# Indirect scatters and gathers in rounds of six with one semaphore, in a fused graph-attention and mixture-of-experts kernel

## The chip, the core and the metric

One core of a Trainium2 chip runs the whole kernel. Its engines are TensorE (matrix products), VectorE, ScalarE, GpSimd (called POOL in the profile) and the sync engine SP, which issues DMAs; all of them have queues of their own and meet only at semaphores. Matrices live in HBM or in the on-chip memory. The metric is the time of one execution on the device in microseconds; the kernel before took 1102.97 us as the median of three runs (1098.57 to 1109.63).

## The reference

The input `x` has 64 batches of 128 tokens with 128 features, float32. Four layers follow each other, each added to `x`:

1. graph attention with 8 heads over the 128 tokens of a batch, on a layer norm of `x`;
2. a shared feed-forward network plus a routed mixture of 8 experts with the best 2 kept per token, on a layer norm of `x`;
3. a second graph network (two attentions with a dense part between);
4. a feed-forward network applied to the tokens with the highest weight in each batch.

The change lies in layer 2:

```python
shared = gelu(x @ W1s + b1s) @ W2s + b2s
rw = softmax(x @ Wr)
topw, topi = top_k(rw, 2)
topw = topw / sum(topw)
...
h = gelu(einsum('bsd,edf->bsef', x, W1p) + b1p)
priv = einsum('bsef,efd->bsed', h, W2p) + b2p
routed = einsum('bsed,bse->bsd', priv, mask)
return shared + routed
```

## The kernel before

**Phases.** The phases run one after the other: setup, attention of layer 1 (ends near 275 us of the span), the experts of layer 2 (to near 647), the graph network of layer 3 (which first adds the experts' results to `x`), and the last feed-forward network. Each phase is a block: no engine starts the next phase before all have ended this one.

**Experts, in words.** The kernel doesn't compute all 8 experts for every token. It sorts the 16384 pairs of token and chosen expert into rows of a table in HBM, `rows_in`, so that each expert's rows stand together, cut into 71 tiles of 256 rows (`TILE`, `TILES`). Each tile belongs to one expert. Its rows are loaded, multiplied by that expert's two matrices, and stored in `rows_out`. Later each token fetches its two result rows.

**Scatter.** POOL fills `rows_in` (`rows_in` and `rows_out` are `slot_rows_in` and `slot_rows_out` in the profile). For each of the 64 batches `b` and both choices `c` one indirect DMA (line 1303) writes the 128 rows of 512 bytes of `xn[:, b]` to the places in `slots`: 128 scatters, numbered `n = 2 * b + c`. Semaphore `scattered[c]` counts those of choice `c`. Before scatter `n`, POOL waits until the scatter before it of the same choice has landed (line 1298), so at most two are under way. At every sixth (`IN_A_ROW`, line 1299) it waits for the other choice too, so that none is under way.

**Chunks.** Eight batches are a chunk, of which there are eight. Whenever a chunk's scatters are known to have landed, POOL runs a small memset (line 1302, the last at 1308) that raises `arrived`. The tiles are worked in an order that puts those first that need only early chunks; row 2 of `tile_table` says how many chunks a tile needs.

**Tile loop.** SP loads tile `t` (`sp_load`, line 1124) six tiles ahead (`AHEAD`), and for `t < 48` (`EARLY`) first waits for the chunks that the tile needs; at `t = 48` it waits for all eight (line 1123) and later no more. Between loads it stores finished tiles (line 1130); its queue is in order, so a wait holds back what is behind it. ScalarE fetches the expert's weights (322 KB, line 957), also about six tiles ahead. TensorE runs per tile: transpose the rows (line 1144) two tiles ahead, the up product (lines 1178 to 1180) one tile ahead, the down product (line 1202). VectorE splits and adds biases, ScalarE applies gelu. While POOL begins to scatter, TensorE works on the shared network (lines 1084 and 1092); the tile loop follows.

**Early gathers.** After its last scatter POOL fetches the result rows of the first 16 batches (`GATHERED_EARLY` chunks of 8) by 32 indirect DMAs (line 1321), with semaphores `early[c]` used as `scattered[c]` is. Before each of the two chunks it waits until the last tile that holds a row of it has been stored (line 1316). The other 96 gathers belong to the next phase (`pool_gather`, line 1597), have semaphores of their own, and are not touched by the change.

Of the kernel before, what the change touches and what calls it, by code (L numbers as in the profile page):

```python
# [14 lines left out]
BATCHES, TOKENS, D = 64, 128, 128  # L15
# [18 lines left out]
def wait(eng, sem, count):  # L34

    if isinstance(count, int) and count <= 0:
        return
    eng.wait_ge(sem, count)
# [887 lines left out]
TOPK = 2  # L926
# [9 lines left out]
CHUNK = 8  # L936
IN_A_ROW = 6
EARLY = 48
CHUNKS = BATCHES // CHUNK
# [5 lines left out]
def slot_rows(k, c, b):  # L945

    return k.xn[:, b, :] if c == 0 else k.xnT[:, (b + 2 * AHEAD * TILE // P) % BATCHES, :]
# [12 lines left out]
def experts_phase(nc, k, a):  # L960

    with ExitStack() as ctx:
        def sb(name, shape, dt=F32):
            return buffer(nc, ctx, name, shape, dt)
# [4 lines left out]
        def sem(name):  # L969
            return ctx.enter_context(nc.semaphore(name))  # L970
# [34 lines left out]
        pool_fence = sb("r_pool_fence", [P, CHUNKS])  # L1005
        EC = GATHERED_EARLY
# [25 lines left out]
        s = {n: sem("m_" + n) for n in (  # L1032
            "iota", "d", "slots", "keys", "marks", "table", "tot_ps", "pre_ps", "key_ps", "tab_ps", "arrived",
            "sh_ps", "sh_ok", "sy_ps", "sy_read", "fold",
            "tp_ps", "xh_ok", "xT_ok", "wh_ok", "wl_ok", "h_ps", "h_ok", "y_ps", "y_ok")}
        rows_kept = sem("m_rows_kept")
        scattered = [sem(f"m_scattered{p}") for p in range(2)]
        early = [sem(f"m_early{c}") for c in range(TOPK)]
        x_in = [sem(f"m_x_in{q}") for q in range(U)]
        out = [sem(f"m_out{q}") for q in range(U)]  # L1040
        READ_PREFIX = 16
# [202 lines left out]
        with nc.Block() as block:  # L1244
            @block.sync
            def _(sp):

                for e in range(EXPERTS):
                    def load(dst, src):
                        sp.dma_start(dst, src, allow_slow_non_contiguous=True).then_inc(k.experts_loaded, 16)  # L1250
                    load(k.b_experts[:, e, 0:FC], a["L0_ffn_b1p"][e].rearrange("(c p) -> p c", p=P))
                    load(k.b_experts[:, e, FC:FC + D], a["L0_ffn_b2p"][e].partition_broadcast(P))
                    load(k.w2_experts[:, e, :].rearrange("p (c n) -> p c n", c=FC),
                         a["L0_ffn_W2p"][e].rearrange("(c p) n -> p c n", p=P))

                sp.dma_start(k.expert_rows[:, :, 0:F], a["L0_ffn_W1p"]).then_inc(rows_kept, 16)
                sp.wait_ge(s["table"], 1)
                sp.dma_start(k.expert_rows[:, :, F:FETCHED].rearrange("e p n -> p e n"), k.b_experts[:])\
                    .then_inc(rows_kept, 16)
                sp.wait_ge(rows_kept, 32)  # L1260
                for t in range(AHEAD):
                    fetch_expert(sp, k, t, t)
                sp.wait_ge(s["sh_ps"], -(-H * U // GB) * FC)
                for t in range(U):
                    sp_load(sp, t)
                for t in range(TILES):
                    if t + U < TILES:
                        sp_load(sp, t + U)
                    sp_store(sp, t)
                for q in range(U):  # L1270
                    sp.wait_ge(out[q], 16 * len(range(q, TILES, U)))

            @block.gpsimd
            def _(pool):
                pool.iota(em8[:], [[1, EXPERTS]], base=-EXPERTS, channel_multiplier=0,
                          allow_small_or_imprecise_dtypes=True)
                pool.iota(k256[:], [[TILE, MAX_TILES_OF_ONE]], base=0, channel_multiplier=0,
                          allow_small_or_imprecise_dtypes=True)
                pool.iota(j_of[:], [[0, 1]], base=0, channel_multiplier=1, allow_small_or_imprecise_dtypes=True)
                pool.iota(j_end[:], [[0, 1]], base=TILE, channel_multiplier=TILE, allow_small_or_imprecise_dtypes=True)  # L1280
                pool.iota(j_start[:], [[0, 1]], base=0, channel_multiplier=TILE, allow_small_or_imprecise_dtypes=True)
                pool.iota(tile_far[:], [[1, TILES]], base=-int(FAR), channel_multiplier=0,
                          allow_small_or_imprecise_dtypes=True)
                pool.iota(order[:], [[1, EXPERTS]], base=0, channel_multiplier=EXPERTS,
                          allow_small_or_imprecise_dtypes=True)
                pool.iota(is_tile[:, EXPERTS, :], [[1, TILES]], base=0, channel_multiplier=0,
                          allow_small_or_imprecise_dtypes=True)
                pool.memset(payload[:, EXPERTS, 0:1], 0.0)
                pool.memset(payload[:, EXPERTS, 1:2], 1.0 / J)
                pool.memset(payload[:, EXPERTS, 2:3], 0.0)  # L1290
                pool.tensor_copy(tri_b[:], k.tri[:])
                pool.tensor_copy(ones_b[:], k.ones[:]).then_inc(s["iota"], 1)

                pool.wait_ge(k.slots_zeroed, 16 * k.zero_dmas)
                pool.wait_ge(s["slots"], 1)
                for n in range(TOPK * BATCHES):
                    b, c = n // TOPK, n % TOPK
                    wait(pool, scattered[c], 16 * b)
                    if n % IN_A_ROW == 0:
                        wait(pool, scattered[1 - c], 16 * b)  # L1300
                    if c == 0 and b % CHUNK == 1 and b > 1:
                        pool.memset(pool_fence[:, b // CHUNK - 1:b // CHUNK], 0.0).then_inc(s["arrived"], 1)
                    pool.indirect_dma_start(  # L1303
                        k.rows_in, bass.IndirectOffsetOnAxis(ap=k.slots[:, c, b:b + 1], axis=0),
                        k.xn[:, b, :], None).then_inc(scattered[c], 16)
                for c in range(TOPK):
                    pool.wait_ge(scattered[c], 16 * BATCHES)
                pool.memset(pool_fence[:, CHUNKS - 1:CHUNKS], 0.0).then_inc(s["arrived"], 1)

                pool.wait_ge(s["table"], 1)  # L1310
                for n in range(TOPK * CHUNK * EC):
                    b, c = n // TOPK, n % TOPK
                    if n % (TOPK * CHUNK) == 0:
                        at = b // CHUNK
                        stored = pool.value_load(last_at[at:at + 1, 0:1], min_val=1 + U, max_val=TILES + U)
                        pool.wait_ge(s["y_ok"], stored)
                        pool.tensor_tensor(gather_fence[:, at:at + 1], k.ones[:, 0:1], k.ones[:, 0:1], ALU.mult)
                    wait(pool, early[c], 16 * b)
                    if n % IN_A_ROW == 0:
                        wait(pool, early[1 - c], 16 * b)  # L1320
                    pool.indirect_dma_start(
                        slot_rows(k, c, b), None, k.rows_out,
                        bass.IndirectOffsetOnAxis(ap=k.slots[:, c, b:b + 1], axis=0)).then_inc(early[c], 16)
                for c in range(TOPK):
                    pool.wait_ge(early[c], 16 * CHUNK * EC)

            @block.scalar
            def _(act):
# [991 lines left out]
def build(nc, a, out):  # L2320

    with ExitStack() as whole:
        k = persistent(nc, whole)
        with ExitStack() as tokens:
            add_token_buffers(nc, tokens, k)
            with ExitStack() as buffers:
                add_attention_buffers(nc, buffers, k)
                setup_phase(nc, k, a)
                head_attention_phase(nc, k, a)
            with ExitStack() as buffers:  # L2330
                add_expert_buffers(nc, buffers, k)
                experts_phase(nc, k, a)
            combine_graph_phase(nc, k)
        last_ffn_phase(nc, k, out)
# [28 lines left out]
```

## Time and profile before

| what | value |
|---|---|
| median of three runs | 1102.97 us |
| lowest, highest run | 1098.57, 1109.63 us |
| profiled execution, whole time | 1114.18 us |
| its span, first to last instruction | 1112.5 us |
| TensorE busy in the span | 974.8 us (88%) |
| POOL busy in the span | 479.2 us (43%) |
| mean granted TensorE clock | 0.957 |

The profile is one execution of its own, and its times add up to its own total, which lies 11.2 us over the median of the three runs. Of that total, 1.7 us lie outside the span. An engine's busy time counts only instructions that work; semaphore waits show up as idle time before the next instruction. An indirect DMA appears on POOL with the time that POOL spends on issuing it, not with the time until its rows have landed; the landing shows in the wait of whoever needed it.

### The profile page before, as it was taken

How to read it: one execution, taken by the hardware profiler on the slowest of the kernel's cores; microseconds unless marked ns; L12 is line 12 of the kernel's file. 1: busy time of each engine (PE TensorE's matmuls, PEld its weight loads, DVE VectorE, ACT ScalarE, POOL GpSimd, SP SyncE). 2: the span in 40 equal slices, each digit the busy share in tenths (PEclk: the TensorE clock that was granted, in tenths of full speed). 3: DMA queues.
4: the chain of work that ended last, by engine and by line, in shares of the span. 5: the costliest groups of instructions: out<-in, count | busy, mean ns of one | idle time of the engine just before them, and what ended most of it. 6: DMA issues, size and time to landing. Idle time of an engine off the chain costs nothing. (4 is left out here: it accounts for less than half of the span.)

```text
span 1112.5 us, 25145 instructions
## 1 busy us (share of the span) xinstructions
PE 974.8 (88%) x7933; PEld 818.3 (74%) x7981; DVE 738.6 (66%) x2240; ACT 677.5 (61%) x1670; POOL 479.2 (43%) x477
## 2 busy tenths in 40 slices
PE   1699999897999999999899957998888998459998
PEld 1578888886677799999899934665556665349997
DVE  4689899885550155554455545788778896569998
ACT  4446666754433456666566625887677787367773
POOL 2556555551155654444444225666656312011111
PEclk9989999997999999999999978999999999679999
DMA  7902222112623146766576510111101000001111
GB/s 201 376 7 115 115 113 113 72 40 79 178 87 105 46 131 201 204 206 194 170 209 202 150 33 24 32 32 29 32 22 35 9 1 1 1 1 38 29 38 48
DMA packets 93001, 103.45 MB, mean 93 GB/s; under 512 B 16480, under 2 KB 69856, under 8 KB 90720
## 3 DMA queue, kind: packets, MB, share of 16 engines
q1 hardware_dynamic: 73232, 59.71, 16.5%
q10 hardware_dynamic: 11472, 25.63, 8.1%
q0 software_dynamic: 8192, 16.79, 5.0%
q8 instruction: 55, 0.90, 0.3%
q14 instruction: 50, 0.41, 0.1%
HBM read 52.54 MB, written 43.27 MB: 86 GB/s over the span
## 5 line engine op out<-in xcount | busy, mean ns | idle before, releaser
L1303 POOL DMA_INDIRECT slot_rows_in<-xn_all,slots x128 | 128.5, 1004 | 136.7 <-DMA slot_rows_in<-xn_all,slots 87.8
L1189 ACT ACTIVATE s_hT<-s_hp,expert 128x256 f32<-128x256 f32 x284 | 114.0, 474 | 72.0 <-PE s_hp L1180 51.2
L1202 PE MATMUL s_yp<-w_experts,s_hT 128*128 x1136 | 139.5, 276 | 1.7 <-issue 1.6
L1202 PEld LDWEIGHTS s_yp<-w_experts,s_hT 128*128 128x128 f32 x1136 | 133.8, 193 | 2.3 <-issue 2.3
L1210 DVE TENSOR_TENSOR xnT_all<-s_yp,expert 128x256 f32<-128x256 f32 x71 | 30.1, 423 | 117.3 <-PE s_yp L1202 87.2
L489 DVE SCALAR_TENSOR_TENSOR l_mi<-l_sbc,mT 128x512 bf16<-128x512 f32 x128 | 84.2, 668 | 5.7 <-PE l_sbc L480 5.0
L1178 PE MATMUL s_hp<-e_xh,e_wh 128*128 128x256 f32 x284 | 86.3, 304 | 0.0
L1101 ACT ACTIVATE s_hT<-s_hp,b_shared 128x512 f32<-128x512 f32 x64 | 44.0, 687 | 65.1 <-PE s_hp L1084 61.8
L1180 PE MATMUL s_hp<-e_xh,e_wl 128*128 128x256 f32 x284 | 80.7, 284 | 0.0
L1179 PE MATMUL s_hp<-e_xl,e_wh 128*128 128x256 f32 x284 | 80.6, 284 | 0.0
L1668 PE MATMUL g_hh<-w_fc,g_r1T 128*128 128x257 f32 x256 | 65.3, 402 | 14.5 <-ACT g_h L1683 9.0
L1767 POOL TENSOR_TENSOR g_u<-g_t,g_r1T 128x1024 f32<-128x1024 f32 x16 | 42.0, 2628 | 70.0 <-DVE g_t L1762 70.0
L1668 PEld LDWEIGHTS g_hh<-w_fc,g_r1T 128*128 128x128 f32 x256 | 48.1, 197 | 27.5 <-ACT g_h L1683 13.3
L1597 POOL DMA_INDIRECT xn_all<-slot_rows_out,slots x48 | 49.0, 1022 | 41.7 <-SPq L2026 23.7
L2161 POOL TENSOR_TENSOR f_wd<-f_wb,ident 128x512 f32<-128x512 f32 x16 | 21.3, 1329 | 100.4 <-ACT f_wb L2155 100.4
L1092 PEld LDWEIGHTS s_yp<-w_shared,s_hT 128*128 128x128 f32 x512 | 59.4, 192 | 6.3 <-issue 6.2
L1160 ACT CAST e_wh<-expert 128x512 fp32r<-128x512 f32 x71 | 44.0, 621 | 28.5 <-issue 28.1
L1084 PE MATMUL s_hp<-xnT_all,w_shared 128*128 128x512 f32 x128 | 59.6, 611 | 1.8 <-PEq L89 1.6
L1092 PE MATMUL s_yp<-w_shared,s_hT 128*128 128x128 f32 x512 | 60.0, 275 | 0.0
L2206 PE MATMUL f_yp<-w_last,f_hT 128*128 128x128 f32 x512 | 59.6, 275 | 0.0
L2206 PEld LDWEIGHTS f_yp<-w_last,f_hT 128*128 128x128 f32 x512 | 58.4, 192 | 0.1
L1597 POOL DMA_INDIRECT xnT_all<-slot_rows_out,slots x48 | 47.7, 994 | 18.6 <-issue 10.7
(336 smaller groups left out, 2689.4 us busy)
## 6 DMA issues: line engine op xcount, KB each, us to landing
expert<-expert_rows ACTq DMA_DIRECT2D x65, 322.0 KB
slot_rows_in<-zeros SPq DMA_DIRECT2D x9, 1024.0 KB, 12.4
xnT_all<-slot_rows_in SPq DMA_DIRECT2D x71, 128.0 KB
slot_rows_out<-xnT_all SPq DMA_DIRECT2D x71, 128.0 KB
slot_rows_out<-zeros SPq DMA_DIRECT2D x8, 1024.0 KB, 4.4
xn_all<-l_xr SPq DMA_DIRECT2D x16, 256.0 KB
xnT_all<-l_rT SPq DMA_DIRECT2D x16, 256.0 KB
out_dram<-f_ot SPq DMA_DIRECT2D x16, 256.0 KB, 2.3
```

What stands on the lines that cost most here:

```text
L489: ins = dve.scalar_tensor_tensor(mi[:, b % 2, 4 * h:4 * h + 4, :], sbc[:, h, :].rearrange("p (q i) -> p q i", q=4), 0.0, k.mT[:].unsqueeze ...
L1084: pe.matmul(hp[:, c, :], k.w1_shared[:, c * P:(c + 1) * P], k.xnT[:, bass.ds(g * GB, GB), :], start=True, stop=True).then_inc(s["sh_ps"], 1)
L1092: ins = pe.matmul(yp[p][:, b * P:(b + 1) * P], s_hT[p][:, c, b * P:(b + 1) * P], k.w2_shared[:, c, :], start=(c == 0 and b == 0), stop=(c ...
L1178: pe.matmul(out_c, wh[q % 2][:, at], xh[q % 2][:], start=True, stop=False)
L1179: pe.matmul(out_c, wh[q % 2][:, at], xl[q % 2][:], start=False, stop=False)
L1180: pe.matmul(out_c, wl[q % 2][:, at], xh[q % 2][:], start=False, stop=True).then_inc(s["h_ps"], 1)
L1189: nc.scalar.activation(hT[q % 2][:, c, :], hp[:, c, 0:TILE], ACT.Gelu, bias=wt[q][:, F + c:F + c + 1]).then_inc(s["h_ok"], 1)
L1202: ins = pe.matmul(yp[q % 2][:, h * D:(h + 1) * D], hT[q % 2][:, c, h * P:(h + 1) * P], w2, start=(c == 0 and h == 0), stop=(c == FC - 1), ...
L1303: pool.indirect_dma_start(k.rows_in, bass.IndirectOffsetOnAxis(ap=k.slots[:, c, b:b + 1], axis=0), k.xn[:, b, :], None).then_inc(scattered ...
L1597: pool.indirect_dma_start(slot_rows(k, c, b), None, k.rows_out, bass.IndirectOffsetOnAxis(ap=k.slots[:, c, b:b + 1], axis=0))\
L1668: ins = pe.matmul(hh[:, b % 2, 0:W1C], r1T[p][:, c, b * P:(b + 1) * P], k.w_fc[:, c, 0:W1C], start=(c == 0), stop=(c == H1 - 1))
L2206: ins = pe.matmul(yp[p][:, b * P:(b + 1) * P], hT[p][:, c, b * P:(b + 1) * P], k.w2_last[:, c, :], start=(c == 0 and b == 0), stop=(c == F ...
```

## The change

The two semaphores per kind become one: `scattered` for all scatters, `early` for all early gathers. The wait before each DMA for its predecessor of the same choice goes away. What is left is one wait ahead of every sixth DMA, for all that were issued before it. So up to six are under way, and then none. The memset that raises `arrived` is now run at the first of these waits at which the chunk is complete: ahead of scatters 18, 36, 48, 66, 84, 96 and 114, in place of 18, 34, 50, 66, 82, 98 and 114. The count of DMAs, their sizes, addresses and order stay the same, and so does everything outside the experts' phase.

```diff
@@ -1034,8 +1034,7 @@
             "sh_ps", "sh_ok", "sy_ps", "sy_read", "fold",
             "tp_ps", "xh_ok", "xT_ok", "wh_ok", "wl_ok", "h_ps", "h_ok", "y_ps", "y_ok")}
         rows_kept = sem("m_rows_kept")
-        scattered = [sem(f"m_scattered{p}") for p in range(2)]
-        early = [sem(f"m_early{c}") for c in range(TOPK)]
+        scattered, early = sem("m_scattered"), sem("m_early")
         x_in = [sem(f"m_x_in{q}") for q in range(U)]
         out = [sem(f"m_out{q}") for q in range(U)]
         READ_PREFIX = 16
@@ -1293,18 +1292,19 @@
 
                 pool.wait_ge(k.slots_zeroed, 16 * k.zero_dmas)
                 pool.wait_ge(s["slots"], 1)
+                arrived = 0
                 for n in range(TOPK * BATCHES):
                     b, c = n // TOPK, n % TOPK
-                    wait(pool, scattered[c], 16 * b)
                     if n % IN_A_ROW == 0:
-                        wait(pool, scattered[1 - c], 16 * b)
-                    if c == 0 and b % CHUNK == 1 and b > 1:
-                        pool.memset(pool_fence[:, b // CHUNK - 1:b // CHUNK], 0.0).then_inc(s["arrived"], 1)
+                        wait(pool, scattered, 16 * n)
+                        if n >= (arrived + 1) * TOPK * CHUNK:
+                            pool.memset(pool_fence[:, arrived:arrived + 1], 0.0).then_inc(s["arrived"], 1)
+                            arrived += 1
                     pool.indirect_dma_start(
                         k.rows_in, bass.IndirectOffsetOnAxis(ap=k.slots[:, c, b:b + 1], axis=0),
-                        k.xn[:, b, :], None).then_inc(scattered[c], 16)
-                for c in range(TOPK):
-                    pool.wait_ge(scattered[c], 16 * BATCHES)
+                        k.xn[:, b, :], None).then_inc(scattered, 16)
+                assert arrived == CHUNKS - 1
+                pool.wait_ge(scattered, 16 * TOPK * BATCHES)
                 pool.memset(pool_fence[:, CHUNKS - 1:CHUNKS], 0.0).then_inc(s["arrived"], 1)
 
                 pool.wait_ge(s["table"], 1)
@@ -1315,14 +1315,12 @@
                         stored = pool.value_load(last_at[at:at + 1, 0:1], min_val=1 + U, max_val=TILES + U)
                         pool.wait_ge(s["y_ok"], stored)
                         pool.tensor_tensor(gather_fence[:, at:at + 1], k.ones[:, 0:1], k.ones[:, 0:1], ALU.mult)
-                    wait(pool, early[c], 16 * b)
                     if n % IN_A_ROW == 0:
-                        wait(pool, early[1 - c], 16 * b)
+                        wait(pool, early, 16 * n)
                     pool.indirect_dma_start(
                         slot_rows(k, c, b), None, k.rows_out,
-                        bass.IndirectOffsetOnAxis(ap=k.slots[:, c, b:b + 1], axis=0)).then_inc(early[c], 16)
-                for c in range(TOPK):
-                    pool.wait_ge(early[c], 16 * CHUNK * EC)
+                        bass.IndirectOffsetOnAxis(ap=k.slots[:, c, b:b + 1], axis=0)).then_inc(early, 16)
+                pool.wait_ge(early, 16 * TOPK * CHUNK * EC)
 
             @block.scalar
             def _(act):
```

## Rows read from the trace of the kernel before

**Rows 1.** The page, its first line.

```profile
span 1112.5 us, 25145 instructions
```

**Rows 2.** Busy time by stretch: stretch, length, busy us per engine.

```profile
340.00:380.00 40.00, 40.00 (x224) 28.52 (x223) 4.15 (x6) 17.03 (x26) 23.09 (x25) 1.00 0.17 54
...
470.00:520.00 50.00, 49.76 (x436) 49.59 (x435) 25.77 (x58) 31.31 (x73) 22.89 (x23) 1.00 0.71 206
```

**Rows 3.** Waits of TensorE from 380 to 647: total us, times, longest.

```profile
PE s_yp L1202 <- issue: 1.6, 3, 1.1
PE r_prefix L1144 <- DVE e_xl L1153: 1.4, 2, 1.1
```

**Rows 4.** Line 1303, the scatters: durations in ns min/median/max, then idle before them.

```profile
L1303 POOL DMA_INDIRECT slot_rows_in<-xn_all,slots x128: 952/958/2168, 299.3 to 550.1; - x128
...
  DMA slot_rows_in<-xn_all,slots: 87.8, 54
```

**Rows 5.** Timeline of POOL, first round of six: start, us, what, [idle before <-releaser].

```profile
299.29 1.21 POOL L1303 DMA_INDIRECT slot_rows_in<-xn_all,slots  x1 [22.73 <-DVE slots L1436]
...
305.85 0.96 POOL L1303 DMA_INDIRECT slot_rows_in<-xn_all,slots  x1 [0.30 <-issue]
308.84 0.96 POOL L1303 DMA_INDIRECT slot_rows_in<-xn_all,slots  x1 [2.03 <-DMA slot_rows_in<-xn_all,slots]
```

**Rows 6.** Timeline of POOL, scatters beside the tile loop.

```profile
414.68 0.96 POOL L1303 DMA_INDIRECT slot_rows_in<-xn_all,slots  x1 [0.59 <-issue]
...
465.29 1.46 POOL L1303 DMA_INDIRECT slot_rows_in<-xn_all,slots  x1 [0.30 <-issue]
469.02 0.95 POOL L1303 DMA_INDIRECT slot_rows_in<-xn_all,slots  x1 [2.27 <-DMA slot_rows_in<-xn_all,slots]
...
537.74 0.95 POOL L1303 DMA_INDIRECT slot_rows_in<-xn_all,slots  x1 [2.76 <-DMA slot_rows_in<-xn_all,slots]
```

**Rows 7.** Timeline of POOL, last fence of the scatters, last early gather, next phase.

```profile
552.40 0.10 POOL L1308 MEMSET r_pool_fence<- 128x1 f32 x1 [1.38 <-DMA slot_rows_in<-xn_all,slots]
...
623.63 0.94 POOL L1321 DMA_INDIRECT xnT_all<-slot_rows_out,slots  x1 [0.30 <-issue]
648.29 0.94 POOL L1597 DMA_INDIRECT xn_all<-slot_rows_out,slots  x1 [23.71 <-SPq L2026]
```

**Rows 8.** Waits of the sync engine's own queue, whole span.

```profile
SPq L1123 <- POOL r_pool_fence L1308: 4.4, 1, 4.4
```

**Rows 9.** Timeline of the sync engine, the load of tile 48 and the next.

```profile
552.73 0.37 SPq L1124 DMA_DIRECT2D xnT_all<-slot_rows_in  x1
...
555.34 0.07 SPq L1124 DMA_DIRECT2D xnT_all<-slot_rows_in  x1
```

**Rows 10.** The page, DMA issues: count, KB each, us from issue to landing.

```profile
slot_rows_out<-zeros SPq DMA_DIRECT2D x8, 1024.0 KB, 4.4
...
out_dram<-f_ot SPq DMA_DIRECT2D x16, 256.0 KB, 2.3
```

**Rows 11.** Timeline of TensorE, the row transposes of tiles 44, 45, 46 and 48.

```profile
541.15 0.38 PE L1144 MATMUL r_prefix<-ident,xnT_all 128*128 128x128 f32 x2
...
548.48 0.41 PE L1144 MATMUL r_prefix<-ident,xnT_all 128*128 128x128 f32 x2 [1.12 <-DVE e_xl L1153]
...
553.48 0.38 PE L1144 MATMUL r_prefix<-ident,xnT_all 128*128 128x128 f32 x2
...
560.42 0.41 PE L1144 MATMUL r_prefix<-ident,xnT_all 128*128 128x128 f32 x2
```

**Rows 12.** Timeline of TensorE, the row transpose of tile 2.

```profile
395.82 0.41 PE L1144 MATMUL r_prefix<-ident,xnT_all 128*128 128x128 f32 x2 [1.07 <-issue]
```

**Rows 13.** Timeline of TensorE, the row transposes of tiles 69 and 70.

```profile
632.54 0.38 PE L1144 MATMUL r_prefix<-ident,xnT_all 128*128 128x128 f32 x2
...
635.97 0.38 PE L1144 MATMUL r_prefix<-ident,xnT_all 128*128 128x128 f32 x2
```

**Rows 14.** DMA queues from 420 to 552: packets, MB, share of 16 engines.

```profile
q0 software_dynamic: 1920, 3.94, 8.5%
```

## The prediction

> **What bounds the kernel now.** I first asked whether POOL, the only engine whose instructions change, is on the path that sets the end. The span [rows 1] is made of stages, so I read the busy times by stretch. Before the tile loop (340 to 380 us), while POOL scatters, TensorE is busy for all 40.00 us; beside the tile loop (470 to 520) for 49.76 of 50 [rows 2]. In both, POOL does about 23 us of issuing and otherwise waits. Next the waits of TensorE over the whole stretch from 380 to 647: the two groups that stand here, of three, are 1.6 and 1.4 us in all, and neither has POOL or a scatter as its releaser [rows 3]. So the experts' phase runs at TensorE's pace, one tile per 3.43 us (635.97 less 632.54 [rows 13]).
>
> Then POOL itself. Its scatters take 0.96 us each to issue and it waits 87.8 us for earlier ones to land [rows 4]. They end with the fence at 552.40. The 32 early gathers follow, the last issued at 623.63. After that POOL idles 23.71 us until the next phase starts at 648.29 [rows 7]. This gap is what the argument rests on: a POOL that finishes sooner only waits longer, since the next phase needs TensorE's last tile and the last store, not POOL.
>
> There are two places at which someone could feel the scatters: the load of tile 48, which waits for all chunks, and contention among DMAs.
>
> **What the change does to the scatters.** Unhindered issues follow each other at 0.96 + 0.30 = 1.26 us [rows 5]. In the first round no wait but the sixth's matters: from 299.29 to 308.84, 9.55 us [rows 5]. Such a round is already what the change makes of every round, so it gains nothing there. Later the two-in-flight wait costs: from 414.68 (scatter 66) to 537.74 (scatter 120) nine rounds take 123.06 us, 13.67 each [rows 6].
>
> With six in a row a round is five steps of 1.26, 6.30 us, and then the time from the sixth issue to the first of the next round. Quiet, that is 308.84 − 305.85 = 2.99 us [rows 5]; beside the tile loop 469.02 − 465.29 = 3.73 us, with two under way [rows 6]. How long it takes with six under way, no row shows. Bounds: at 2.99 a round is 9.29 us and the scatters end at 299.29 + 21.3 rounds, about 498 us; if six in flight drain no faster in total than two, nothing is gained and they end at 552. I take the loaded row, since that is the stretch where the waits are: 6.30 + 3.73 = 10.03 us. The first eleven rounds (299.29 to 414.68, 10.49 each) at 9.55 end at 404; the other 10.3 rounds at 10.03 end at **508 us**, some 44 us sooner. By the Trainium skill (DMA: Bandwidth & Descriptors, "Anatomy of one DMA — SWDGE (gpsimd) path") a DMA issued from GpSimd costs a fixed 2.0 us plus its bytes at 436 GB/s, 2.15 us for these 64 KB, counted from its issue. That would put a round at 8.45 us and the end near 480; the quiet row shows 2.99 and the loaded one 3.73, more than the page allows, and the trace decides.
>
> **The early gathers.** 32 of them are 5.3 rounds. From 552.40 to 623.63 they take 71.2 us, 2.2 each, like the loaded scatters [rows 7]. At 10 to 13.7 us per round they take 53 to 73 us and can start at 508, so POOL is done between 561 and 581 in place of 625, unless the wait for a stored tile holds them. POOL's gap before 648.29 grows from 24 to between 67 and 87 us. None of it reaches the end: **0 us**. What hides it is the rest of the tile loop; that cover would go only if POOL were later than today by 23 us.
>
> **Waits removed and added.** About 160 semaphore waits go from POOL's stream; at most part of the 0.30 us between issues, off the path: 0. The added wait stands at the head of each round. Queued behind it are the round's six issues and at times a fence. The fences of chunks 2 and 5 come two scatters later in number (at 36 and 84, 34 and 82 before), 2.5 us of issuing; two others come earlier. But scatter 36 now comes at 299.29 + 6 × 9.55 = 356.6 us, and the late rounds are 3.6 us shorter each, so no fence is later in time. On SP only one wait for a fence shows at all, the one for all chunks [rows 8], so the earlier ones have slack. SP's stores behind it are needed only six tiles later. DMAs: same number, same bytes, same order; their queues are not passed by any other.
>
> **The load of tile 48.** SP waits 4.4 us for the last fence [rows 8] and issues the load at 552.73 [rows 9]; TensorE transposes that tile at 560.42 [rows 11]. In this execution there is room, because TensorE had just lost time: from 541.15 to 553.48, two tiles take 12.33 us in place of 6.86, a stall of 5.47 us [rows 11] whose releaser isn't POOL. Without that stall tile 48 would be due at 541.15 + 4 × 3.43 = 554.87. The load's landing isn't shown. The nearest rows are 2.3 us for 256 KB and 4.4 us for 1 MB [rows 10]; so it lands at 555.0 to 557.1, that is 0.2 to 2.3 us late. In an execution without the stall the change thus saves 0.2 to 2.3 us; with it about 0 (it can't lose, as the fence comes earlier). I take 1 us, near the smaller transfer. After the change the load goes out at its own time, 552.73 − 4.4 = 548.3 or sooner.
>
> **Sum.** Profiled execution: 1114.18 − 0 (scatters) − 0 (gathers) − 0 (waits) − 0 to 1 (tile 48) = 1113 to 1114. It stands 11.2 us over the median, of which the stall may be 5.5. On the median: 1102.97 − 1 = **1102 us**.
>
> **Rivals.** *The slow scatters cause TensorE's lost time.* Between tile 2 at 395.82 [rows 12] and tile 70 at 635.97 [rows 13] lie 68 steps, 240.15 us; at 3.43 they are 233.2, so 6.9 us are lost. If all of it hangs on late rows, it goes: 1103 − 6.9 = 1096; with a lucky run more. For it: the largest loss, 5.47 us, lies in the last rounds of the scatters. Against it: no row of TensorE's waits names one, and SP's only wait for a fence begins at 548.3, when the stall is half over.
>
> *The rounds of six get in the way of the tile loop (slower).* Place: the DMA engines, where a backlog of up to six scatters or gathers meets tile loads (line 1124) and weights (957). A late one makes the up product wait. Beside the tile loop run about 10 rounds of scatters and 6 of gathers. If each costs TensorE a wait of the size of those it has, 1.6 / 3 = 0.53 us [rows 3], that is 8.5 us: 1111.5; at the longest one, 1.1 us, it is 17.6 us: 1120.6. It decides from the point where a load lands later than its room: tile 48's was 560.42 − 552.73 = 7.7 us even after SP's wait, 12 us without it, against 2.3 to 4.4 for landing. Against it: the software queue holds only 8.5% of the engines' time there [rows 14], and the bytes stay the same; POOL's slack would have to become TensorE's loss. The Trainium skill (DMA: Bandwidth & Descriptors, "Queues, rings and completion order") says that each DMA engine takes turns between the queues that have work, a packet at a time. By that rule a queue that always has a backlog takes its turn each time, which speaks for this rival; no row here shows the turns.
>
> *The depth doesn't take effect.* Six in flight drain one after the other, rounds stay at 13.7 us and the scatters end near 550: 1103, no change.
>
> **How the numbers follow.** A measurement of this kernel tells about 1% (11 us) from no change. Forecast (POOL off the path, 1102): 60%. Depth without effect (1103): 10%. Lost time given back (1096): 14%, of which 6 points pass 1%. Contention (1111.5): 16%, of which 8 points pass 1%. Drift of the three runs between 1098.57 and 1109.63 adds 2 points on either side. That makes faster 8%, slower 10%, same 82%. The range runs from 1094, the first rival with 2 us of drift, to 1111, the lower price of contention; outside stay the larger price and larger drifts, under 20%. The forecast's own range is 1098 to 1107.
>
> **What would show it.** Line 1303: no wait within a round; rounds near 10 us from 410 on; last fence near 508 (498 to 552). The wait at line 1123 gone. POOL's idle time before line 1597 over 50 us. TensorE's step 3.43 us and its last row transpose within a few us of 636. The prediction is wrong if TensorE's waits between 396 and 644 grow by more than 5 us, if lost time there vanishes wholly, or if anything before 299 or after 648 changes by more than the runs differ.

## The result and the profile after

The changed kernel took 1157.80 us as the median of four runs (1155.47 to 1160.66), the kernel before, beside it, 1103.85 us (1098.57 to 1109.63). The ratio is 1.0471, 95% interval 1.0415 to 1.0527: **slower by 4.7%**, where I had forecast 1102 and a range of 1094 to 1111. What follows found that this holds for some of the occasions on which the two kernels ran and not for others; so this section reads the trace of that first comparison, and the next one tells the occasions apart. Medians here are of all runs; ratios and intervals leave out a few runs that the record marks as slow, among them two of the kernel before in the second group of experiments, at 1427.06 and 2469.34 us, of which no trace is kept.

The page of the changed kernel, first line and busy times (us, share, instructions):

```profile
span 1158.9 us, 25165 instructions
...
PE 993.8 (86%) x7981; PEld 828.3 (71%) x7981; DVE 741.7 (64%) x2240; ACT 674.3 (58%) x1670; POOL 479.0 (41%) x477
```

The span grew by 46.4 us [rows 1], TensorE's busy time by 19.0. Timeline of POOL in the changed kernel: the last fence of the scatters, the last early gather, the first DMA of the next phase.

```profile
510.50 0.10 POOL L1308 MEMSET r_pool_fence<- 128x1 f32 x1 [2.15 <-DMA slot_rows_in<-xn_all,slots]
...
572.96 0.94 POOL L1320 DMA_INDIRECT xnT_all<-slot_rows_out,slots  x1 [0.30 <-issue]
...
705.46 0.94 POOL L1595 DMA_INDIRECT xn_all<-slot_rows_out,slots  x1 [131.56 <-SPq L2024]
```

These answer to [rows 7]. POOL did just what was forecast: scatters over at 510.50, 202.9 us after the first at 307.63 (253.1 before), gathers over at 574. Its idle time before the next phase grew from 23.71 to 131.56 us. That is more than the 67 to 87 forecast, because the tile loop ended late. Row transposes of TensorE in the changed kernel, for tiles 2, 21, 36 and 70:

```profile
406.31 0.41 PE L1143 MATMUL r_prefix<-ident,xnT_all 128*128 128x128 f32 x2 [3.22 <-DVE e_xl L1152]
...
510.59 0.38 PE L1143 MATMUL r_prefix<-ident,xnT_all 128*128 128x128 f32 x2
...
576.40 0.38 PE L1143 MATMUL r_prefix<-ident,xnT_all 128*128 128x128 f32 x2
...
693.13 0.38 PE L1143 MATMUL r_prefix<-ident,xnT_all 128*128 128x128 f32 x2
```

Tile 2 to tile 70 takes 286.8 us, 240.15 before [rows 12, 13]; 68 steps of 3.43 would be 233.2. The loss of 53.6 us has a sharp edge. Tile 2 to 21, while POOL scatters: 19 steps, 104.3 us, 39.1 lost. Tile 21 to 36, while it gathers: 15 steps, 65.8 us, 14.3 lost. Tile 36 to 70, POOL idle: 34 steps, 116.7 us, nothing lost. What lies outside the tile loop nearly cancels: the first scatter comes 8.3 us later than before (307.63 against 299.29), the stretch from there to tile 2 is 2.2 us longer, and all after tile 70 is 10.8 us shorter. So the 46.7 us of the tile loop are the result. For the same matmuls, from tile 2 to tile 70, the changed kernel and then the kernel before (stretch, its length, TensorE busy and count, granted clock, DMA share, GB/s):

```profile
406.31:693.13 286.82, 253.87 (x2040) 0.96 0.55 158
```

```profile
395.82:635.97 240.15, 236.79 (x2040) 0.99 0.66 191
```

Of the 46.7 us, 29.6 are time in which TensorE is idle (32.95 less 3.36), and 17.1 are time in which it is busy for longer with the same work, at a granted clock of 0.96 in place of 0.99.

Who waited? Waits of VectorE from 395 to 720 in the changed kernel (us in total, times, longest), first

```profile
DVE xnT_all L1209 <- PE s_yp L1201: 104.0, 53, 6.9
DVE xnT_all L1209 <- remote: 52.9, 15, 6.9
```

and of ScalarE:

```profile
ACT s_hT L1188 <- remote: 53.6, 15, 6.7
```

The kernel before has the same two rows in small, which I had not read before the prediction. VectorE:

```profile
DVE xnT_all L1210 <- remote: 13.4, 3, 6.8
```

and of the same kernel's ScalarE:

```profile
ACT s_hT L1189 <- remote: 5.1, 2, 4.2
```

TensorE's own waits in the changed kernel, same stretch, which answer to [rows 3]:

```profile
PE r_prefix L1143 <- DVE e_xl L1152: 13.6, 8, 3.2
...
PE s_hp L1177 <- ACT s_hT L1188: 7.6, 7, 2.1
PE s_yp L1201 <- issue: 7.2, 14, 1.1
```

All six rows of that view add up to about 36 us, close to TensorE's idle time, and none of them has a DMA as releaser: no tile and no weights came late. "Remote" in the rows of VectorE and ScalarE is where the profile sees the semaphore rise but no instruction that ended then. The timeline shows why. One stall in the changed kernel, all engines, 420 to 429 us:

```profile
420.24 0.96 POOL L1303 DMA_INDIRECT slot_rows_in<-xn_all,slots  x1 [3.02 <-DMA slot_rows_in<-xn_all,slots]
...
421.50 0.96 POOL L1303 DMA_INDIRECT slot_rows_in<-xn_all,slots  x1 [0.30 <-issue]
...
421.87 1.95 PE L1201 MATMUL s_yp<-w_experts,s_hT 128*128 x16
...
422.77 0.96 POOL L1303 DMA_INDIRECT slot_rows_in<-xn_all,slots  x1 [0.30 <-issue]
...
423.65 0.38 PE L1143 MATMUL r_prefix<-ident,xnT_all 128*128 128x128 f32 x2
...
425.29 0.96 POOL L1303 DMA_INDIRECT slot_rows_in<-xn_all,slots  x1 [0.30 <-issue]
425.30 0.98 PE L1201 MATMUL s_yp<-w_experts,s_hT 128*128 x6
425.89 0.69 SPq L1123 DMA_DIRECT2D xnT_all<-slot_rows_in  x1
426.56 0.96 POOL L1303 DMA_INDIRECT slot_rows_in<-xn_all,slots  x1 [0.31 <-issue]
...
427.34 0.36 PE L1201 MATMUL s_yp<-w_experts,s_hT 128*128 x1 [1.05 <-issue]
...
428.75 1.06 PE L1201 MATMUL s_yp<-w_experts,s_hT 128*128 x8 [0.43 <-issue]
...
428.85 0.42 DVE L1209 TENSOR_TENSOR xnT_all<-s_yp,expert 128x256 f32<-128x256 f32 x1 [6.88 <-remote]
429.00 1.20 ACT L1188 ACTIVATE s_hT<-s_hp,expert 128x256 f32<-128x256 f32 x3 [4.93 <-remote]
429.05 0.96 POOL L1303 DMA_INDIRECT slot_rows_in<-xn_all,slots  x1 [1.53 <-DMA slot_rows_in<-xn_all,slots]
```

TensorE ends a down product at 423.8 (it starts at 421.87 and takes 1.95), which should release VectorE; ScalarE waits for up products, which run from 423.79 on. The two start at 428.85 and 429.00. In the trace's record of semaphore updates every update by a compute engine stops at 422.31 and comes back at 428.83, then five of them within 0.2 us; only increments by DMAs arrive in between. TensorE runs on for a while, then issues in drips from 427.34. POOL's third scatter of the round starts at 422.77, and its next round at 429.05, when the six have landed. So for 6.5 us the engines' work was done but nobody was told, and this ends as the round drains. Gaps of over 3 us between such updates, from 395 to 720, number 10 in the changed kernel and 3 in the kernel before, the longest of which (541.09 to 546.49) is the stall of [rows 11].

The stalls have an aftermath. The trace's records of the granted clock show the lower level (1.2 GHz, half speed) from 407.68 to 411.09, 438.39 to 445.22, 465.70 to 469.11, 472.53 to 475.94 and twice more. Five of the six begin within 8 us of the end of such a gap; the gap before the second lasts from 430.68 to 437.56. A down product in it takes 3.21 us, against the 1.95 of the same one above:

```profile
442.57 3.21 PE L1201 MATMUL s_yp<-w_experts,s_hT 128*128 x16
```

The kernel before has one such stretch in its tile loop, 548.89 to 552.31, right after its longest gap.

SP's wait for the last fence [rows 8] did go, as forecast: no row names line 1308. What shows is a wait for the second fence, from 355.80 to 364.81, before the tile loop.

```profile
SPq L1123 <- POOL r_pool_fence L1301: 9.0, 1, 9.0
```

### The profile page after: what moved, and what is told of

Read it like the earlier page. It is cut to its first block and busy times, and to the rows that moved or that the text cites. A ratio compares the mean times of both kernels' runs of the same rounds, so it can differ in the third digit from the quotient of the medians.

```text
span 1158.9 us, 25165 instructions
## 1 busy us (share of the span) xinstructions
PE 993.8 (86%) x7981; PEld 828.3 (71%) x7981; DVE 741.7 (64%) x2240; ACT 674.3 (58%) x1670; POOL 479.0 (41%) x477
## 5 line engine op out<-in xcount | busy, mean ns | idle before, releaser
L1201 PE MATMUL s_yp<-w_experts,s_hT 128*128 x1136 | 146.3, 282 | 7.7 <-issue 7.2
L1201 PEld LDWEIGHTS s_yp<-w_experts,s_hT 128*128 128x128 f32 x1136 | 139.3, 198 | 10.3 <-issue 10.2
L1177 PE MATMUL s_hp<-e_xh,e_wh 128*128 128x256 f32 x284 | 89.2, 314 | 11.0 <-ACT s_hT L1188 7.6
L1666 PE MATMUL g_hh<-w_fc,g_r1T 128*128 128x257 f32 x256 | 61.8, 386 | 10.2 <-ACT g_h L1681 6.6
L1177 PEld LDWEIGHTS s_hp<-e_xh,e_wh 128*128 128x128 f32 x284 | 55.8, 196 | 14.3 <-ACT s_hT L1188 7.5
L1666 PEld LDWEIGHTS g_hh<-w_fc,g_r1T 128*128 128x128 f32 x256 | 46.2, 190 | 22.6 <-ACT g_h L1681 10.8
```

The costliest lines, as they stand in the source:

```text
L1177: pe.matmul(out_c, wh[q % 2][:, at], xh[q % 2][:], start=True, stop=False)
L1201: ins = pe.matmul(yp[q % 2][:, h * D:(h + 1) * D], hT[q % 2][:, c, h * P:(h + 1) * P], w2, start=(c == 0 and h == 0), stop=(c == FC - 1), ...
L1666: ins = pe.matmul(hh[:, b % 2, 0:W1C], r1T[p][:, c, b * P:(b + 1) * P], k.w_fc[:, c, 0:W1C], start=(c == 0), stop=(c == H1 - 1))
```

## The experiments

The 18 kernels ran in six groups, each beside the kernel before on the same chip. Groups differ more than kernels do. The kernel before took 1095.83, 1097.48, 1099.33 and 1098.52 us in four of them; I call these quiet. In two, and in the first comparison, it took 1103.85 to 1115.57; I call these held. The sign in the traces is the gap in the engines' semaphore updates: over 3 us long, it occurs 3 times in each held trace of the kernel before (without and with the copies of the fourth group) and 10 to 16 times with six in flight on held occasions, and never, from 395 to 640, in the fourteen quiet traces. (A result names its chip by a number: quiet 3, 2, 6 and 1, held 9 and 3. Number 3 is on both sides; whether it is one chip, the results don't tell.)

Two more things part the occasions. The scatters and early gathers make 160 × 16 = 2560 increments. The quiet traces hold records of 2469 to 2535 of them; the held ones of 753 to 918 with six in flight, and of 1435 and 1517 with two. So on held occasions the record of updates is itself full of holes. And behind tile 70, where nothing was changed, the held traces take 465.8 to 476.5 us (the kernel before 476.5) and the quiet ones 459.5 to 463.7; what makes that difference is open. The DMAs themselves are no slower: from 402 to 552 a 4096-byte packet of the software queue takes 189 ns on average in the held trace of the changed kernel and 199 in the quiet one.

| kernel | occasion | median us | before, same group | ratio, 95% interval |
|---|---|---|---|---|
| changed | held (first) | 1157.80 | 1103.85 | 1.0471 (1.0415 to 1.0527) |
| changed | held | 1177.01 | 1106.88 | 1.063 (1.0446 to 1.0815) |
| six in flight, six semaphores | held | 1165.35 | 1115.57 | 1.0465 (1.032 to 1.061) |
| before + copies | held | 1125.94 | 1106.88 | 1.0169 (1.0098 to 1.024) |
| changed + copies | held | 1182.26 | 1106.88 | 1.0678 (1.0581 to 1.0774) |
| changed | quiet | 1095.84 | 1097.48 | 1.0004 (0.9965 to 1.0043) |
| changed | quiet | 1099.01 | 1099.33 | 0.9999 (0.9955 to 1.0044) |
| six, six semaphores | quiet | 1095.82 | 1095.83 | 1.0002 (0.9965 to 1.0039) |
| six, six semaphores, again | quiet | 1099.68 | 1099.33 | 0.9955 (0.9906 to 1.0005) |
| six, two semaphores | quiet | 1094.68 | 1097.48 | 0.9948 (0.9899 to 0.9998) |
| depth 4 | quiet | 1095.16 | 1095.83 | 0.9986 (0.9945 to 1.0028) |
| depth 3, twice | quiet | 1096.17, 1097.20 | 1095.83, 1098.52 | 1.0003, 0.9969 |
| half rows, twice | quiet | 1095.99, 1098.57 | 1095.83, 1098.52 | 0.9992, 1.0018 |
| scatters only | quiet | 1095.45 | 1097.48 | 0.999 (0.9943 to 1.0037) |
| gathers only | quiet | 1097.39 | 1097.48 | 0.9989 (0.9941 to 1.0037) |
| six only beside the shared network | quiet | 1095.14 | 1099.33 | 0.9962 (0.9916 to 1.0007) |
| sixteen in a row | quiet | 1095.70 | 1099.33 | 0.9952 (0.9927 to 0.9977) |

**First group: depth against one semaphore.** Two theories for the held updates: more than two indirect DMAs in flight hold them (depth), or the 96 increments of a round to one semaphore do. Rings of semaphores, here with three, four or six:

```diff
-        scattered, early = sem("m_scattered"), sem("m_early")
+        scattered = [sem(f"m_scattered{p}") for p in range(RING)]
...
+                    wait(pool, scattered[n % RING], 16 * (n // RING))
                     pool.indirect_dma_start(
...
-                        k.xn[:, b, :], None).then_inc(scattered, 16)
+                        k.xn[:, b, :], None).then_inc(scattered[n % RING], 16)
```

> Six in flight as in the changed kernel, but each of the six has a semaphore of its own, and the wait ahead of a round is for all six semaphores. Theory depth (more than two indirect DMAs in flight hold back the semaphore updates of the compute engines until they have landed; 18 tile steps of 5 to 8.7 us in place of 3.43): stays slow, 1150 to 1162 us. Theory one semaphore (the 96 increments of a round meet at one semaphore): back near the kernel before, 1100 to 1110 us.

> Four semaphores in turn, so at most four scatters or early gathers in flight, and none at every sixth as in both kernels. Theory depth: between the two kernels, 1115 to 1150 us, with fewer long tile steps than the 21 of the changed kernel. Theory one semaphore: 1100 to 1110 us. Theory that the drain at the head of a round does the harm (it is in all kernels alike): no change from the kernel before.

> Three semaphores in turn, at most three in flight. Theory depth: if the loss grows with each DMA past two, about 1110 to 1125 us; if it is a threshold near six, 1104 as before. Theory one semaphore: 1100 to 1110 us.

```diff
-                        k.rows_in, bass.IndirectOffsetOnAxis(ap=k.slots[:, c, b:b + 1], axis=0),
-                        k.xn[:, b, :], None).then_inc(scattered, 16)
+                        k.rows_in, bass.IndirectOffsetOnAxis(ap=k.slots[0:64, c, b:b + 1], axis=0),
+                        k.xn[0:64, b, :], None).then_inc(scattered, 16)
```

> The changed kernel, but each scatter writes only the first 64 of its 128 rows; the other rows of the table stay zero (this part of the computation is left out). Gathers are whole. The count of scatters, their order and their increments stay. If the rows and bytes written hold up the semaphores, the stalls get shorter by about half: 1125 to 1140 us. If the number of DMAs with their 16 increments does, it stays at 1150 to 1160 us. If nothing but the time in flight counts, POOL's issue (0.96 us) may get shorter too, and the landing sooner: below 1125 us.

All four came out at 1095 to 1096 us, no slower than the kernel before; half rows, which leaves out half of the rows, too. For three this looked like a verdict against the one semaphore, but half rows has one semaphore as well. The busy times of the six-semaphore kernel from 402 to 552 (stretch, its length, then busy us and count of TensorE, its weight loads, VectorE, ScalarE, POOL; granted clock, DMA share, GB/s) show TensorE full:

```profile
402.00:552.00 150.00, 149.89 (x1310) 149.92 (x1311) 78.37 (x175) 95.44 (x219) 81.24 (x86) 1.00 0.73 203
```

Without the changed kernel itself in the same group, nothing could be concluded. That control was missing, and was next.

**Second group: the control.**

> The changed kernel unaltered, as a control, on the chip and in the hour of the kernels beside it. Six semaphores, depth 4, depth 3 and half rows all ran at 1096 us like the kernel before, with none of the long gaps between semaphore updates. Theory one semaphore: this one is slow again, 1140 us or more, with some 20 long tile steps. Theory depth can only stand if the place of the run matters (another chip or another hour): then this is 1090 to 1105 us here, without gaps, and the 4.7% belong to where the first comparison ran.

> The changed kernel with two semaphores in place of one per kind, scatters of either choice on their own, the wait for both at the head of each round; six in flight. Theory one semaphore: 1096 us, or between if the number of increments per semaphore matters (48 in place of 96): 1100 to 1130 us. Theory place of the run: 1090 to 1105 us.

> Only the scatters as in the changed kernel; the early gathers keep their two semaphores and two in flight. In the changed kernel 16 of the 21 long gaps lie in the time of the scatters. Theory one semaphore: most of the loss, 1130 to 1150 us. Theory place of the run: 1090 to 1105 us.

> Only the early gathers as in the changed kernel; the scatters as before. Theory one semaphore: a small loss, 5 to 15 us, 1101 to 1111 us. Theory place of the run: 1090 to 1105 us.

```diff
# six_two_sems: scattered and early are lists of two again
-                        wait(pool, scattered, 16 * n)
+                        for p in range(2):
+                            wait(pool, scattered[p], 16 * (n // 2))
# scatters_only: the early gathers' lines are those of the kernel before
# gathers_only: the scatters' lines are those of the kernel before
```

The unaltered changed kernel ran at 1095.84 us, ratio 1.0004. First its row, then, for the same stretch, the changed kernel's of the first comparison, and the one of the kernel before there:

```profile
402.00:552.00 150.00, 150.00 (x1314) 150.00 (x1313) 77.31 (x173) 95.25 (x219) 82.41 (x90) 1.00 0.72 206
```

```profile
402.00:552.00 150.00, 118.53 (x883) 111.44 (x881) 53.57 (x119) 64.97 (x150) 85.36 (x92) 0.93 0.51 147
```

```profile
402.00:552.00 150.00, 146.65 (x1257) 145.43 (x1257) 76.61 (x170) 92.92 (x212) 68.95 (x72) 0.99 0.68 197
```

In the quiet run TensorE is busy for 150.00 of 150 us, in the held one for 118.53, with the granted clock at 0.93 in place of 1.00. Tiles 2 and 70 of the quiet run:

```profile
400.40 0.41 PE L1143 MATMUL r_prefix<-ident,xnT_all 128*128 128x128 f32 x2 [1.07 <-DVE e_xl L1152]
...
633.89 0.38 PE L1143 MATMUL r_prefix<-ident,xnT_all 128*128 128x128 f32 x2
```

233.5 us for 68 steps is 3.43 each, busy throughout at a granted clock of 1.00: the tile loop loses nothing. POOL of that run, last fence of the scatters and first DMA of the next phase:

```profile
517.47 0.10 POOL L1308 MEMSET r_pool_fence<- 128x1 f32 x1 [1.32 <-DMA slot_rows_in<-xn_all,slots]
...
646.22 0.94 POOL L1595 DMA_INDIRECT xn_all<-slot_rows_out,slots  x1 [70.83 <-SPq L2024]
```

So on a quiet occasion the kernel behaves as I had forecast, down to POOL's gap of 70.83 us (67 to 87 forecast) and the scatters, over 213.6 us after the first (209 forecast). One semaphore by itself costs nothing here; what remained was that the occasion matters, and on a held one depth and the one semaphore were still both possible. Scatters only and gathers only told nothing on such an occasion.

**Third group: the same again, and a greater depth.**

> The changed kernel once more, unaltered. Two chips have now run it or its relatives at 1096 us without a long gap between semaphore updates; the first comparison found 1158 against 1104. If what held the updates back belongs to a certain chip or its neighbours' work, the result depends on where this lands: 1096 again, or some 1150 us with gaps of 3 to 7 us during the rounds of six.

> Six in flight with six semaphores, to stand beside the changed kernel wherever this lands. If that one is slow here, theory depth says this is slow too (within 10 us of it); theory one semaphore says it is at the time of the kernel before. If that one is not slow, this tells nothing new: 1096 us.

> Rounds of six only for the first 60 scatters, which run beside the shared network; from then on two semaphores and two in flight as in the kernel before, for the early gathers too. On a chip without gaps: 1096 us. On one with gaps: theory depth says the tile loop is spared, within 1% of the kernel before, since the gaps beside the shared network cost TensorE nothing there (both traces take 89.9 us from the first scatter to the first row transpose).

```diff
# a ring of two; in the scatters' loop
+                    if n >= 60:
+                        wait(pool, scattered[n % RING], 16 * (n // RING))
```

> The changed kernel with sixteen in a row in place of six, eight waits in all for the scatters. Theory depth in its general form (a backlog of scatters holds back the semaphore updates on any chip, only the depth at which it begins differs): over 1110 us and long gaps also on a chip where six does nothing. If a backlog does nothing by itself: 1090 to 1100 us, scatters over near 490 us.

```diff
-IN_A_ROW = 6
+IN_A_ROW = 16
```

Quiet again. Sixteen in flight do no harm either; the row of that kernel:

```profile
402.00:552.00 150.00, 148.93 (x1302) 148.72 (x1301) 77.93 (x174) 95.67 (x220) 89.93 (x96) 1.00 0.75 205
```

So a backlog by itself doesn't hold the updates; the occasion has to bring something too. The ratio of that kernel, 0.9952, is no gain to build on: two others of the same group, one of them with rounds of six beside the shared network only, stand at 0.9955 and 0.9962.

**Fourth group: load, and luck.**

```diff
# load_before, load_after: behind each tile's store
                     sp_store(sp, t)
+                    sp.dma_start(scratch_rows[t], a["x"][2 * (t % 32):2 * (t % 32) + 2]).then_inc(moved, 16)
```

> The kernel before plus one copy of 128 KB from HBM to HBM per tile, issued by SP behind the tile's store (it adds work that the output doesn't use). It raises the load on the DMA engines and on HBM during the tile loop, from a share of 0.72. It is the partner of the next run: whatever the copies cost by themselves shows here. Estimate 1096 to 1130 us.

> The changed kernel plus the same copies. Theory loaded memory (six scatters in flight hold back the semaphore updates where something else loads HBM, as a neighbour may have on the first chip): at least 15 us over its partner, with gaps of over 3 us between the compute engines' semaphore updates. Theory that the cause is not to be had by load from this core: within 1% of its partner, no such gaps.

> The changed kernel unaltered, for the chip of this call. 1096 to 1099 us if this chip is like the last three; some 50 us over the kernel before, with gaps, if it is like the first.

This group was held. The unaltered changed kernel took 1177.01 us against 1106.88, 6.3% slower, so the first result was no accident of that comparison. Its row, then its VectorE's wait:

```profile
402.00:552.00 150.00, 118.74 (x834) 112.04 (x835) 52.22 (x115) 61.50 (x141) 76.83 (x84) 0.89 0.49 137
```

```profile
DVE xnT_all L1209 <- remote: 77.7, 16, 7.7
```

The copies cost the kernel before 19.1 us, mostly as a plain wait for tile loads,

```profile
PE r_prefix L1146 <- DMA xnT_all<-slot_rows_in: 13.5, 13, 1.8
```

and the changed kernel with copies is 56.3 us over its partner. That fits the number expected of the theory of load, but doesn't support it: without copies the changed kernel is 70.1 us over the kernel before in the same group, so the copies did not bring the held updates. The rows of the two, before with copies and changed with copies:

```profile
402.00:552.00 150.00, 138.82 (x1181) 135.57 (x1179) 71.80 (x158) 88.21 (x200) 64.78 (x69) 1.00 0.75 209
```

```profile
402.00:552.00 150.00, 110.95 (x748) 102.65 (x747) 46.50 (x102) 54.64 (x123) 80.57 (x87) 0.85 0.52 142
```

The question that the pair was made for, whether load brings the stalls on a quiet occasion, is not answered.

**Fifth group: depth or semaphore, on a held occasion.**

> Six in flight, six semaphores, once more. Two of five chips so far (the first comparison's and the last one's) show the changed kernel 4.7% and 6.3% slower and the kernel before at 1104 to 1107 us; on three the kernel before is at 1096 to 1099 us and nothing changes. If this call's chip is of the slow kind: theory depth 1150 to 1180 us with a dozen gaps or more; theory one semaphore 1104 to 1110 us. On a chip of the quick kind: 1096 us, which tells nothing.

Held again: 1165.35 us against 1115.57. Its row and its VectorE's wait:

```profile
402.00:552.00 150.00, 119.24 (x882) 113.31 (x881) 53.02 (x119) 66.37 (x150) 87.47 (x96) 0.91 0.52 147
```

```profile
DVE xnT_all L1216 <- remote: 93.3, 16, 7.9
```

Sixteen of VectorE's waits again, as many as in the changed kernel of the fourth group, and gaps of over 3 us between the engines' updates number 16 here and 11 there. TensorE is at 119.24 of 150 us. The edit keeps the depth and gives each DMA in flight a semaphore of its own, and nothing is won. So on a held occasion the shared semaphore isn't what costs. What the slow forms share is the round itself: up to six in flight, issued 1.26 us apart without a wait. Depth and pace were not parted. The kernel before reaches the same pace in its early rounds, with two in flight, and four of its seven gaps between 290 and 720 lie there (336.71 to 390.56).

**Last group: what of the depth.**

> Three in flight, three semaphores, if possible on a chip of the slow kind (kernel before at 1104 us or more), where six in flight with six semaphores was 1165 us against 1116. Theory depth with a loss that grows with each DMA past two: 1115 to 1140 us and some 5 to 10 gaps over 3 us in the tile loop. If it is a threshold between three and six: within 1% of the kernel before, at most 3 gaps. On a chip of the quick kind: 1096 us.

> The changed kernel with scatters of 64 rows in place of 128 (half of the rows are left out and stay zero), if possible on a chip of the slow kind. If the rows not yet written are what holds the updates back: half the loss or less, 1110 to 1140 us, fewer and shorter gaps. If it is the number of DMAs in flight: 1150 to 1180 us.

Quiet: 1097.20 and 1098.57 us against 1098.52. Neither told anything new. Whether three in flight are safe on a held occasion, and whether rows or DMAs count, stays open.

## Why the prediction was wrong

**Right: POOL is off the path.** Its scatters ended 203 us after the first (forecast 209), its early gathers at 574 (forecast 561 to 581), and SP's wait for the last fence is gone. From the sixth issue to the next round it takes 2.5 us in the held trace and, beside the tile loop, 2.6 to 4.7 in the quiet one, around the 3.73 that I took from a row with two in flight; that the held sum is so near is partly luck. On a quiet occasion the forecast holds: ratios of 1.0004 and 0.9999, where I had 1102/1103.

**Right, but too small to see: tile 48.** The 1 us would be a ratio of 0.999; no interval here is narrow enough.

**Wrong: the zero for what the scatters do to the tile loop, and the slower rival's price and mechanism.** The sum put scatters and gathers at 0 us, with "what hides it is the rest of the tile loop"; on a held occasion that cover is what they hurt. The rival had 16% of the chance, its place was right (rounds of six beside the tile loop, scatters and gathers, some 16 rounds) and so was the point that the loss ends with them. The failing term is the loss per round. I took it from TensorE's own waits, 0.53 us with 1.1 as the upper end [rows 3], which gave 8.5 to 17.6 us. Measured it was 46.7 us over the kernel before, about 2.9 per round: 29.6 of idle TensorE and 17.1 of longer busy time, for which the rival had no term at all. And what held TensorE up was no late tile or weights: it was held semaphore updates. My bound of 7.7 us of room for a tile load was of no use against that. The Trainium skill's rule that the DMA engines take turns between queues (DMA: Bandwidth & Descriptors, "Queues, rings and completion order"), which I had counted for this rival, would have shown as tile loads that release TensorE late; the trace has none.

**The row that I misread.** The stall of 5.47 us [rows 11] was in front of me. I noted that its releaser was not POOL, put it in the profiled run's account, and set it aside. It was one instance of the very mechanism, at two in flight: VectorE and ScalarE both released by "remote" in the middle of a round of scatters. Priced by that row, one such stall in each of 16 rounds, the rival would have been at 1103 + 16 × 5.47 = 1190 us, too much against the measured 1157.80 but on the right side of it, and the range would have had to reach there. I took the mean of the small waits and not the row that fitted the situation. Nor did the stall account for the 11.2 us over the median as I had it: against a quiet trace of the changed kernel that profiled run is 6.7 us longer in the tile loop and 16.9 behind it.

**Shown and not shown.** Shown: on held occasions rounds of six cost 4.7 to 6.3%, with updates of the compute engines' semaphores that stop for 3 to 8 us while a round is in flight, and with a lower granted clock after that; one or six semaphores are alike; on quiet occasions neither six nor sixteen in flight cost anything. Not shown: what makes an occasion held. It may be the chip, or something else that works on it at the time; copies from this core were not tried on a quiet one. Nor is it shown what holds an update back. One rival stands untested: every run on record comes with a span and a granted clock, so each was recorded by the profiler, and held traces lack up to 71% of the increments of the indirect DMAs. Whether the recording takes part in the hold, and whether a run without it would lose the same time, no run tells.

## What to carry to other kernels

When several engines wait at once, and the profile names no instruction as the releaser, look at what is in flight at that time and price a change that adds to it by that one stall, not by the average wait. A queue that isn't on the path can still hurt those that are, so don't deepen it for a gain that the path cannot take: on held occasions the kernel with two in flight was itself 0.4 to 1.8% slower than on quiet ones, and six cost another 4.7 to 6.3% there and nothing elsewhere. And before explaining a slowdown, run the unaltered kernel once more beside the first experiments; I ran four without it, and for one group they seemed to prove the wrong theory.

## What the runs showed of the hardware

- Semaphore updates by TensorE, VectorE and ScalarE can stop all together for 3 to 8 us while indirect DMAs are in flight (422.31 to 428.83 above), and then arrive in a burst. Updates by DMAs go on meanwhile.
- TensorE goes on issuing in that time until it stalls as well: from 423.8 to 425.9 at full pace, then single matmuls at 427.34 and 428.05.
- After such stalls the granted clock falls to its lower level for 3.4 to 6.8 us at a time (438.39 to 445.22 above); of the 53.3 us by which the held tile loop is longer than the quiet one, 20.4 are longer busy time for the same 2040 matmuls (253.87 against 233.49 us).
- Beside the shared network the gaps do less harm, but not none: the first scatter to the first row transpose takes 89.86 us in both kernels of the first comparison (299.29 to 389.15, 307.63 to 397.49), though updates were held for up to 6.8 us (366.73 to 373.52), and 94.87 us in the changed kernel of the fourth group, with ten gaps there. The expectation of the kernel with six only beside the shared network took the first two as the rule.
- With six indirect scatters issued 1.26 us apart, the first of the next round starts 2.50 us after the sixth (314.19 to 316.69), less than the 2.99 us with at most two in flight [rows 5].
